# First cross attention: the output projection of seven token tiles among the last row's weighted sums

## The reference, cut to what matters

```python
def _L0_xattn_ref(q, k, v, w_q, w_k, w_v, w_o):          # k and v: the context, 16 x 1601 x 256
    qp, kp, vp = (_split_head(a @ w) for a, w in ...)    # 16 heads of 16 features
    scores = jnp.einsum('bhqd,bhkd->bhqk', qp, kp) / jnp.sqrt(jnp.float32(d_k))
    ...                                                  # scores that are exactly 0 are masked
    attn = jax.nn.softmax(scores, axis=-1)
    out = jnp.einsum('bhqk,bhkd->bhqd', attn, vp)
    return out.transpose(0, 2, 1, 3).reshape(B, S, H * dh) @ w_o

x = x + _L0_xattn_ref(_layernorm(x, axis=-1), ctx_1024, ctx_1024, ...)
```

## Time and profile before

| what | value |
| --- | --- |
| median of 3 runs | 3747.0 us (3744.45 to 3750.06) |
| profiled execution, time | 3741.22 us |
| profiled execution, span from the first to the last instruction | 3739.4 us |
| PE busy, share of the span | 91% |
| DVE, ACT, POOL busy | 54%, 45%, 19% |
| mean granted TensorE clock | 0.952 of full speed |
| steps of `softmax_context` | some 96 to 742.6 us of the span |
| `project_blocks` of this part, with what surrounds it | 742.6 to 761.7 us |

### The profile page before, as it was taken

How to read it: one execution, slowest core, us unless ns; L and a number is a source line. 1 busy time by engine, 2 the same in 40 slices (tenths; PEclk the granted TensorE clock), 3 DMA queues, 4 the chain that set the end, 5 groups by cost and what they waited for, 6 DMA issues and landing times. The chain is left out here.

```text
span 3739.4 us, 90592 instructions
## 1 busy us (share of the span) xinstructions
PE 3392.7 (91%) x39440; PEld 2399.7 (64%) x39440; DVE 2029.0 (54%) x4106; ACT 1691.4 (45%) x3093; POOL 701.6 (19%) x343
## 2 busy tenths in 40 slices
PE   6999999879998979999879998999999789998975
PEld 4677667656775658888754455777776555554544
DVE  4666766653443357777655483565656443333337
ACT  3776777623332167887635452444444331111222
POOL 0777677410110000000031021101110000000001
PEclk9999999889998989999988999999999879999986
DMA  1111111030101424344010002111110013220610
GB/s 64 54 38 38 37 40 53 2 99 25 40 1 41 135 74 171 109 165 160 16 37 15 0 1 68 43 55 40 58 40 21 24 34 108 93 73 9 246 48 16
DMA packets 155253, 223.53 MB, mean 60 GB/s; under 512 B 39375, under 2 KB 134539, under 8 KB 154732
## 3 DMA queue, kind: packets, MB, share of 16 engines
q1 hardware_dynamic: 154860, 217.75, 17.5%
HBM read 216.67 MB, written 1.05 MB: 58 GB/s over the span
## 5 line engine op out<-in xcount | busy, mean ns | idle before, releaser
L3225 POOL TENSOR_TENSOR x_sc<-x_sc,h_T 128x2048 f32<-128x2048 f32 (+1 forms) x105 | 443.3, 4270 | 223.7 <-ACT h_T L3436 223.7
L3041 ACT ACTIVATE x_sc<-x_sc,x_nb 128x2048 f32<-128x2048 f32 (+1 forms) x112 | 210.6, 1880 | 297.7 <-DVE x_sc L3090 297.6
L3090 DVE SCALAR_TENSOR_TENSOR x_sc<-ps,x_nb,x_cap 128x2048 f32<-128x2048 f32 (+1 forms) x112 | 246.2, 2199 | 49.3 <-PE ps L2982 49.3
L3510 DVE TENSOR_TENSOR x_most<-x_most,ps 128x512 f32<-128x512 f32 (+1 forms) x352 | 234.8, 685 | 61.8 <-PE ps L3342 35.8
L1736 ACT ACTIVATE s1i_both<-ps,s_less,s_rs_s 128x64 f32<-128x64 f32 x624 | 214.5, 428 | 47.8 <-DVE s_less L1853 47.8
L3415 ACT COPY x_sc<-ps 128x1024 f32<-128x1024 f32 x192 | 179.1, 942 | 89.2 <-PE ps L3342 51.3
L3429 ACT ACTIVATE x_sc<-x_sc 128x2048 f32<-128x2048 f32 (+1 forms) x112 | 200.6, 1792 | 26.0 <-POOL x_sc L3225 21.9
L3298 PE MATMUL ps<-x_wv,x_ctx_T 128*128 128x256 f32 (+1 forms) x832 | 202.8, 385 | 0.0
L2953 PE MATMUL ps<-x_ctx_T,x_wk 128*128 128x401 f32 (+1 forms) x512 | 200.0, 518 | 1.5 <-PEq L44 1.5
L3290 PE MATMUL ps<-x_ctx_T,x_wk 128*128 128x401 f32 (+1 forms) x512 | 194.7, 518 | 3.4 <-POOL x_v L3254 3.4
L2961 PE MATMUL ps<-x_wv,x_ctx_T 128*128 128x256 f32 (+1 forms) x832 | 197.7, 379 | 0.0
(11 more groups left out here) (518 smaller groups left out, 6925.9 us busy)
## 6 DMA issues: line engine op xcount, KB each, us to landing
x_ctx_T<-in_ctx_T SPq DMA_DIRECT2D x32, 1601.0 KB
s1i_ctx_T<-in_ctx_T SPq DMA_DIRECT2D x16, 1601.0 KB, 7.2
x3i_ctx_T<-in_ctx_T SPq DMA_DIRECT2D x16, 1601.0 KB, 7.3
s1i_ctx_n<-in_ctx SPq DMA_DIRECT2D x16, 1536.0 KB
x3i_ctx_n<-in_ctx SPq DMA_DIRECT2D x16, 768.0 KB
h<-in_ctx SPq DMA_DIRECT2D x12, 896.0 KB
e_w<-in_L_attn_W SPq DMA_DIRECT2D x8, 1024.0 KB, 7.7
rows<-in_ctx SPq DMA_DIRECT2D x12, 640.0 KB
```

The lines of the kernel that those rows point to most:

```text
L3041: nc.scalar.activation(x, x, ACT.Square, scale=DH ** -0.5, bias=nb[0:keys, 0:1]).then_inc(squared, 1)
L3090: nc.vector.scalar_tensor_tensor(out=slot[0:keys].rearrange("p r m h j q -> p (r m h) (j q)")[:, :, 0:width], in0=score_banks[0:keys].rear ...
L3225: return eng.tensor_tensor(x, x, most_of, ALU.subtract)
L3510: ins = nc.vector.tensor_tensor(best[0:keys, rs], best[0:keys, rs], score_banks[0:keys, rs, :, j, :], ALU.max)
```

## The change

The projection of `x0` moves into `softmax_context`. `project(t)` makes the same four matmuls for a tile. PE does tiles 0 to 6 in steps 112 to 118, each between the fillers of the step's middle and the weighted sums; it does tile 7 after the last denominators. Seven products lie in the four score banks, two in a bank, and the eighth in the bank of the weighted sums. DVE adds the seven products to x after its last step and ahead of the last row's divisions, and adds the eighth after them. The block of `project_blocks` is gone from this part (the third layer's cross attention still uses it).

```diff
-            softmax_context(nc, env, "x0", d, ctx_T, q_T, att, top_bc, wk, wv, sc, sbi)
-        project_blocks(nc, env, "x0_o", [part[:, c, :] for part in att for c in range(2)], wo,
-                       env.x)
+            softmax_context(nc, env, "x0", d, ctx_T, q_T, att, top_bc, wk, wv, wo, sc, sbi)
...
+    blocks = [part[:, c, :] for part in att for c in range(2)]
+
+    def product_of(t):
+        return ps[:, t // 2, t % 2 * D:(t % 2 + 1) * D] if t < T - 1 else ps[:, UNIT_BANK, 0:D]
...
+                def project(t):
+                    pe.wait_ge(att_out, 2 * (2 * t + 2))
+                    if t == 0:
+                        pe.wait_ge(copied, 2 * ALL)
+                        pe.wait_ge(maxed, 2 * ALL)
+                    for k, rows in enumerate(blocks):
+                        last = nc.tensor.matmul(product_of(t), rows[:, t * P:(t + 1) * P],
+                                                w_o[:, k, :], start=(k == 0),
+                                                stop=(k == len(blocks) - 1))
+                    last.then_inc(projected, 1)
...
                     for f in middle(n):
                         filler(f)
+                    if ALL <= n < ALL + T - 1:
+                        project(n - ALL)
                     if n >= PV_LAG:
                         values(n - PV_LAG)
                     for f in late(n):
                         filler(f)
                 for f in last_fillers:
                     filler(f)
+                project(T - 1)
...
+                for t in range(T - 1):
+                    dve.wait_ge(projected, min(t // 2 * 2 + 2, T - 1))
+                    nc.vector.tensor_tensor(env.x[:, t, :], env.x[:, t, :], product_of(t),
+                                            ALU.add).then_inc(added, 1)
                 for f in last_fillers:
                     divide(f)
+                dve.wait_ge(projected, T)
+                nc.vector.tensor_tensor(env.x[:, T - 1, :], env.x[:, T - 1, :],
+                                        product_of(T - 1), ALU.add).then_inc(added, 1)
```

More of the change, by code:

```diff
@@ L3127, in _, with softmax_context @@
                 divide(("den", B - 1, 0))
-def softmax_context(nc, env, stage, d, ctx_T, q_T, att, top_bc, w_k, w_v, sc, sb):
+def softmax_context(nc, env, stage, d, ctx_T, q_T, att, top_bc, w_k, w_v, w_o, sc, sb):
     UNITS = [list(range(t, min(t + 2, CT))) for t in range(0, CT, 2)]
@@ L3211, in softmax_context @@
              "terms_turned top_turned brought top_ready shifted shifted_last exped pv_done k_done "
-             "k_taken v_done v_taken u_taken den_done att_out")
+             "k_taken v_done v_taken u_taken den_done att_out projected "
+             "added")
     with signals(nc, stage, names) as (
@@ L3215, in softmax_context @@
             terms_ready, terms_turned, top_turned, brought, top_ready, shifted, shifted_last,
-            exped, pv_done, k_done, k_taken, v_done, v_taken, u_taken, den_done, att_out):
+            exped, pv_done, k_done, k_taken, v_done, v_taken, u_taken, den_done, att_out,
+            projected, added):
         ctx_in = (ctx_even, ctx_odd)
```

## The result

The changed kernel took 3728.7 us (median of 4 runs, 3724.73 to 3731.15) against 3748.5 us before; the ratio is 0.9952, with a 95% interval of 0.9940 to 0.9964. The two medians differ by 19.8 us; the ratio on record, which is not their plain quotient, stands for 18.0 us of 3747. The forecast was 15.

A forecast was written before the change was run, and what follows sets the result against it. PE bounds the 18.4 us projection block, and DVE is nearly full in the drain before it. Walks gave gains of 16.4, 14.8, 14.5 and about 12 us; taking 15, 3747.0 - 15 = 3732 us, range 3725 to 3739.

The forecast's parts named there:

- The price of a tile and the covers: PE per projection tile: 1.72 us at the upper clock, 3.45 at the lower; tile 0 fits a 3.10 us gap free.
- Tile 1: Ahead of the value projection DVE awaits: no delay of DVE's copy at the upper clock, 1.6 us at half clock.
- Tiles 2 and 3: In the drain of the attention: DVE's reciprocal starts 0.8 us later, the only delay that reaches the end.
- The end of the drain: Last weighted sums: better clock gives back 0.8 us and 0.3 more, so they end at 738.4 to 738.8.
- The additions: Seven on DVE ahead of the last reciprocal: 3.0 us, hidden in 5.01 us of idle time, about 0.7 to spare.
- Behind the division: Only tile 7 and its addition remain after the last division: 2.45 us at the upper clock, 4.2 at the lower.
- The signs: Wrong if the last sums end after 742, additions delay the last reciprocal, or a stage after 762 grows.
- The rule on the clock: PE in the drain: dense matmuls keep the clock up, gain 16.4 us; by the rows as they stand, 14.8.
- The slow clock throughout: Half clock while the tiles are in the drain: 4 us slower, about 3751 us; chance 0.04.
- PE as the bound for a part: PE limits part of the drain at half clock: gain only 5 to 12 us; chance 0.15.
- That nothing changes: The next stage or a later one gives the time back: 3747 us; chance 0.05.
- The walk with the clock up: Following PE, ACT and DVE through the drain at the upper clock: end at 744.6 against 761.03, gain 16.4 us.

The follow-up runs named there:

- late-tiles kernel: Against the changed kernel, tiles 1 to 6 stand behind the step's late fillers instead of ahead of the weighted sums; ratio to before 0.9954.
- with the clock held up: Against the changed kernel, PE makes five unread matmuls into an unused bank between the last denominators and tile 7; ratio to before 0.9955.
- the profile with a fast tile 1: Second profile of the unchanged changed kernel, where tile 1 met the upper clock level; the ratio of its set to before is 0.9950.
- The doubled tiles: Against the changed kernel, tiles 0 to 6 are each projected twice in place, 12.0 us of PE work added; ratio to before 0.9968.
- where tile 7 was padded: Against the changed kernel, tile 7 is projected eight times before its addition, 12.0 us of PE work added; two sets, ratios to before 0.9977 and 0.9971.
- the kernel that has it back: Against the changed kernel, tile 7 and its addition go into a block of their own behind the attention; ratio to before 0.9957.

## Why the prediction was right, point by point

**The price of a tile and the covers.** As predicted. Tile 0 fits, with 1.43 us of PE's idle time left (3.10 - 1.72 = 1.38 by the forecast's numbers). The block boundary is 0.6 to 0.7 us net; my sum had it in the 18.4 us without a figure of its own.

**Tile 1** was forecast at 0 at the upper clock and 1.6 us at the lower. It measured 0.1 and 1.9, and the late-tiles kernel shows that under the lower clock its place is what costs.

**Tiles 2 and 3** were forecast at 0.8 us. At the upper clock the reciprocal is 1.2 us later than before, seen from the maximum (21.38 against 20.17). The term was too small: denominators come 0.54 us after DVE is ready there, and DVE also waits for the last value projection (0.42 us in the first profile).

**The end of the drain** was forecast at 0 to 0.3 us earlier at the upper clock. In that profile it is 34.06 against 34.01 us. In the two others it is 1.85 us later, where the walk had 1.7.

**The additions**: 2.39 us, forecast 3.0, with 1.22 us left of the cover, forecast 0.7.

**Behind the division**: forecast 2.45 us, or 4.2 at the lower clock. Measured 4.29, 3.34 and 4.29, and 2.50 with the clock held up. In none of the three was tile 7 wholly at the upper level, so the forecast's 16.4 us did not occur.

**The signs.** The prediction named them in times of the span. By those, one sign of being wrong came true: the last sums ended at 744.04, after 742. But the first profile began its drain 3.46 us later than before; counted from the last maximum the sums ended at 740.6 on the clock of the kernel before, and the last addition at 748.4 (745.7 in the profile with a fast tile 1), where 745 to 747 was named. The reciprocal of step 115 was 3.0, 1.2 and 3.0 us later, not 0.8. The last reciprocal came at 741.7, where no later than about 741.5 was named, though no addition delayed it. DVE's copy stayed within 2 us, and the granted clock in 714 to 739, so counted, rose from 0.73 to 0.93, 1.00 and 0.93.

**The rule on the clock.** By the rule that the prediction took from the Trainium skill ("TensorE: Matmul & The Clock Gate", section "HAM oscillation — how this bites in real kernels") the inserted tiles would hold the clock up. They did so from tile 2 to the end of the drain, which before had run at half speed from 729.4. They did not under tile 1 in two of three profiles.

**The rivals.** The slow clock throughout, and PE as the bound for a part, did not occur with one copy of the tiles. The doubled tiles show that the second was near: the slack that I worked out for PE behind the maxima was 1.7 us, and by that run it was some 1.1 us (12.0 less 9.5, less the 1.4 left ahead of the maxima). That nothing changes is excluded by the intervals.

**The size.** By the stretch the gain was 12.5 us in the mean, the low end of my 12 to 17. The walk with the clock up had 16.4 us. From there 0.8 us go because the base of 18.4 was the slower of two draws of the projection's clock (16.8 in the other), 1.5 because tile 7 ran mostly at half clock, 1.3 because the last division ended later than walked in two of three profiles, and 0.2 with the longer meeting. The 15 us lay between that walk and the slower ones. The timed gain was 12.7 to 18.7 us in three sets. The stretch alone would have put the median at 3734.6, 2.6 us above the forecast; it came out at 3728.7, 3.3 below. That both lie so near 3732 is partly luck: the sum of the steps was somewhat too large, and something outside them took off more.

**What stays open** is that something. Take for each kernel (1 - ratio) x 3747 us, and subtract what its stretch is below 56.3 us, the mean of before. That leaves 1 to 7 us for each changed kernel (18.0 - 11.6 for the first set), and 10 and 13 us where tile 7 was padded. The boundary is not it, since the kernel that has it back shows 5 us of the kind. Stages elsewhere take different times from one execution to the next, by some 5 us and without an edit, so a few profiles can't place it. I have no run that shows the cause.

Three things on record narrow it down. First, the profiled executions do not show it: their mean is 3743.0 us before (two) and 3731.9 for the changed kernel (three), 11.1 us less, no more than the stretch. Outside the stretch the span has 3682.4 and 3687.5 us before, and from 3673.7 to 3695.8, with a mean of 3684.2, in the twelve profiles of changed kernels. Second, what varies there goes with TensorE's clock: 353 us of the next part (821.8 to 1174.8 before), in which the clock stays at 1.00, take 352.97 to 353.02 us in all fourteen profiles, while the feed-forward stage above takes 135.9 to 142.2 us with 13 to 26 us at the lower level. Third, so do the timed runs: within each kernel's set, 0.001 more of mean granted clock goes with 2.4 us less (correlation -0.90 over all sets), and the padded sets had a mean clock of 0.9541 and 0.9540, against 0.951 and 0.950 of the kernel before, measured beside them. The better clock within the stretch makes up 0.0016 of that (10.2 us at the lower level there, against 22.2 in the mean of before). What is left, 0.0014 to 0.0020, would be 3 to 5 us by that slope (an estimate), a part of the 10 and 13. Why the clock elsewhere should be higher stays open.

## What to carry to other kernels

Work that depends only on early results can be handed to the gaps of a pipeline's drain. Count those gaps at both clock levels first; and put the work behind the jobs for which the engine on the critical chain waits, not ahead of them. Two profiles of the unchanged kernel are worth more than a longer look at one: the stretch that was to be removed itself varied by 1.5 us. Where the last piece depends on two results that come one after the other, start half of it on the first.

## What the runs showed of the hardware

TensorE's clock went with most of the variation. A tile was 1.72 us at 2.4 GHz and about twice that at 1.2 GHz (3.55 us, with some start-up, for the first tile of the kernel before). The level fell during 2.4 us in which PE waited for the division, behind 20.94 of 24.3 us of work at the upper level, and 2.32 us of matmuls that nobody reads kept it up. Nor was the pattern fixed: identical code met different levels at the same place in different executions.

A DVE instruction can spend its time waiting and show it as its own duration. In the changed kernel the conversion of 128 x 4 numbers takes 3.47 us right beside POOL's last subtraction, which ends at 714.87, and 0.17 us for the same shape once POOL is idle:

```profile
698.85 16.02 POOL L3229 TENSOR_TENSOR x_sc<-x_sc,h_T 128x2048 f32<-128x2048 f32 x4
...
711.43 3.47 DVE L3546 CAST x_terms<-x_top 128x4 bf16<-128x4 f32 x1
...
716.14 0.17 DVE L3546 CAST x_terms<-x_top 128x4 bf16<-128x4 f32 x1
```

The Trainium skill ("SBUF — State Buffer", section "Who interferes with whom") describes a pair of ports that VectorE and GpSimd share, taken by one of them for a whole instruction. The ends of the two rows, 714.90 and 714.87, agree with that. In the kernel before the same conversion takes 3.43 us. In one of the fourteen profiles, the second of the changed kernel, the time is split: 1.08 us for the conversion and 2.30 us for the subtraction of 128 x 4 numbers behind it, which ends at 715.32, 0.03 us after POOL. These 3.3 us lie on the way to the last row's maxima, in both kernels. No run here tried to avoid them.
